# Slot lists of a GNN kernel: the prefix sum folds its columns twice, GpSimd subtracts the pairs of keys and clears two buffers

## The reference

```python
edge_index = jnp.stack([src, dst])
x = _layernorm(x + _L0_gnn_ref(x, edge_index, edge_weight, ...))        # GCN
x = _layernorm(x + _L1_gnn_ref(x, edge_index, edge_type_8, ...))        # gated, 2 rounds, 8 edge types, GRU
x = _layernorm(x + _L2_gnn_ref(x, edge_index, ...))                     # attention, 8 heads
x = _layernorm(x + _L3_gnn_ref(x, edge_index, edge_attr_64, ...))       # message MLP, mean over a node's edges
```

## Time and profile before

| | us |
|---|---|
| median of 3 runs | 11,153.66 |
| the profiled execution | 11,158.11 |
| its span | 11,156.3 |
| VectorE busy | 5,403.2 (48% of the span) |
| PE busy | 6,170.2 (55%) |
| ScalarE busy | 1,478.6 (13%) |
| GpSimd busy | 4,854.9 (44%) |

### The profile page before, as it was taken

How to read it: one execution, slowest core, us unless ns; L and a number is a source line. 1 busy time by engine, 2 the same in 40 slices (tenths; PEclk the granted TensorE clock), 3 DMA queues, 4 the chain that set the end, 5 groups by cost and what they waited for, 6 DMA issues and landing times. The chain is left out here.

```text
span 11156.3 us, 168161 instructions
## 1 busy us (share of the span) xinstructions
PE 6170.2 (55%) x61543; PEld 5314.1 (48%) x61544; DVE 5403.2 (48%) x7212; ACT 1478.6 (13%) x4112; POOL 4854.9 (44%) x5699
## 2 busy tenths in 40 slices
PE   4666659995433333343333333576899625554554
PEld 3333339994233233333333333575899624444444
DVE  7888878884311111121222222798888643323333
ACT  3666640000100000000000000121000011101111
POOL 1111100001277777767777777001000027777775
PEclk7777779997666666666666666555999857777777
DMA  1000032222222222222222121564322112222222
GB/s 45 0 0 0 0 50 81 85 82 88 81 66 65 53 65 66 65 71 53 52 52 52 52 52 52 190 258 181 107 93 91 60 44 71 78 79 78 78 78 72
DMA packets 323557, 804.89 MB, mean 72 GB/s; under 512 B 157650, under 2 KB 196348, under 8 KB 303772
## 3 DMA queue, kind: packets, MB, share of 16 engines
q1 hardware_dynamic: 148380, 429.92, 11.5%
q0 software_dynamic: 153216, 312.49, 10.8%
q10 hardware_dynamic: 21888, 61.54, 1.4%
HBM read 721.60 MB, written 81.99 MB: 72 GB/s over the span
## 5 line engine op out<-in xcount | busy, mean ns | idle before, releaser
L973 POOL DMA_INDIRECT ggnn_edges_G<-trans_d,ggnn_edges_rid x3136 | 2983.3, 951 | 1318.0 <-issue 955.6
L1077 PE MATMUL ggnn_edges_PS<-ggnn_edges_OH,ggnn_edges_G 128*128 128x128 f32 x6272 | 1177.3, 373 | 2323.9 <-DMA ggnn_edges_G<-trans_d,ggnn_edges_rid 2213.7
L1077 PEld LDWEIGHTS ggnn_edges_PS<-ggnn_edges_OH,ggnn_edges_G 128*128 128x128 f32 x6272 | 1137.0, 284 | 2368.8 <-issue 2368.8
L973 POOL DMA_INDIRECT mpnn_edges_G<-msg_d,mpnn_edges_rid x1568 | 1500.6, 957 | 741.2 <-issue 474.1
L1042 DVE TENSOR_TENSOR acc<-acc,ggnn_edges_PS 128x128 f32 x224 | 64.7, 289 | 2518.1 <-PE ggnn_edges_PS L1077 2518.1
L618 ACT ACTIVATE prep_OJF<-prep_OJ,prep_fld 128x98 bf16<-128x98 bf16 x3136 | 849.0, 362 | 575.2 <-DVE prep_OJ L674 575.2
L1061 PE MATMUL mpnn_edges_PS<-wt_late,mpnn_edges_at 128*128 128x256 f32 x1568 | 545.0, 521 | 681.0 <-DVE mpnn_edges_G L1029 338.4
L1061 PEld LDWEIGHTS mpnn_edges_PS<-wt_late,mpnn_edges_at 128*128 128x128 f32 x1568 | 414.7, 272 | 792.5 <-DVE mpnn_edges_G L1029 359.0
L822 PE MATMUL prep_PS<-prep_OJF,prep_OHr 128*128 128x490 bf16 x1582 | 582.5, 550 | 225.7 <-DVE prep_OHr L701 225.7
L1029 DVE TENSOR_TENSOR mpnn_edges_G<-mpnn_edges_G,mpnn_edges_PS 128x1792 f32<-128x1792 f32 x112 | 226.3, 2021 | 878.4 <-DMA mpnn_edges_G<-msg_d,mpnn_edges_rid 696.1
L1007 DVE SCALAR_TENSOR_TENSOR ggnn_edges_OH<-dstI,ggnn_edges_itm,ggnn_edges_PS 128x896 f32<-128x896 f32 x448 | 491.6, 1144 | 230.4 <-issue 164.7
(11 more groups left out here) (449 smaller groups left out, 10511.7 us busy)
## 6 DMA issues: line engine op xcount, KB each, us to landing
ba_rows<-slot_d SPq DMA_DIRECT2D x50, 3136.0 KB, 11.3
HB<-slot_d SPq DMA_DIRECT2D x50, 1568.0 KB
heads_rows<-slot_d SPq DMA_DIRECT2D x50, 1568.0 KB
ggnn_edges_G<-trans_d,ggnn_edges_rid POOLq DMA_INDIRECT x3136, 2.5
mpnn_edges_at<-in_edge_attr SPq DMA_DIRECT2D x112, 448.0 KB, 4.1
trans_d<-gcn_edges_tb ACTq DMA_DIRECT2D x49, 512.0 KB, 2.6
trans_d<-ggnn_edges_tb ACTq DMA_DIRECT2D x49, 512.0 KB, 3.0
mpnn_edges_G<-msg_d,mpnn_edges_rid POOLq DMA_INDIRECT x1568, 2.5
```

The lines of the kernel that those rows point to most:

```text
L973: pool.indirect_dma_start(G[:, s, c, :], None, table, bass.IndirectOffsetOnAxis(ap=rid[:, s, c:c + 1].bitcast(U32), axis=0)).then_inc(gath ...
L1077: mm = pe.matmul(wp[s % 2], G[:, s, c, :], OH[:, s % 2, c, :], start=c == 0, stop=c == GC - 1)
```

## The change

- The `twin` comparison is split. GpSimd subtracts each pair of keys (14 x 14, f32 out of bf16), after VectorE has signalled `key2` through the new semaphore `keyed`; `key2` has two buffers for that. VectorE then does the comparison with zero and the mask in one instruction and the sum in another, in a new function `same_key`, called at the end of the item, behind `window_hot`. Both are `own.step`.
- The reduce over 98 columns is preceded by two additions in place, of columns 50 to 97 onto 0 to 47 and of 26 to 49 onto 0 to 23, both bf16; the reduce then reads 26 columns.
- GpSimd clears `OJF` and `X` at the start of the stage. ScalarE, PE and VectorE wait for `fields_blank`, VectorE for `recs_blank` as well.

```diff
--- before.py
+++ after.py
@@ -508,7 +508,7 @@
             wm = sb(ctx, "prep_wm", [P, 2, 4, GC], BF16)
             w2 = sb(ctx, "prep_w2", [P, 2, 3, GC, 2], BF16)
             fld = sb(ctx, "prep_fld", [P, 2, 2, GC])
-            key2 = sb(ctx, "prep_key2", [P, GC, 2], BF16)
+            key2 = sb(ctx, "prep_key2", [P, 2, GC, 2], BF16)
             win = sb(ctx, "prep_win", [P, GC], I32)
             twin = sb(ctx, "prep_twin", [P, GC, GC])
             lower = sb(ctx, "prep_lower", [P, GC, GC])
@@ -544,8 +544,11 @@
             product, done, chain, final, turned, dsq, rooted, tidy, hscaled, stored, listed, filled, copied, cleared, over_ready = sems(
                 "prep", "product done chain final turned dsq rooted tidy hscaled stored listed filled copied cleared over_ready")
             totalled, slots_out, begun, taken = sems("prep", "totalled slots_out begun taken")
-            KEY_STEPS, RANK_STEPS, ADD_STEPS = 5, 6, 2
-            STEPS = KEY_STEPS + RANK_STEPS + ADD_STEPS
+            fields_blank, recs_blank = sems("prep", "fields_blank recs_blank")
+            keyed, diffed = sems("prep", "keyed diffed")
+            KEY_STEPS, RANK_STEPS, ADD_STEPS = 2, 8, 2
+            SAME_STEPS = 2
+            STEPS = KEY_STEPS + RANK_STEPS + ADD_STEPS + SAME_STEPS
             with nc.Block() as block:
                 @block.sync
                 def _(sp):
@@ -575,6 +578,8 @@
 
                 @block.gpsimd
                 def _(pool):
+                    nc.gpsimd.memset(OJF[:], 0.0).then_inc(fields_blank, 1)
+                    nc.gpsimd.memset(X[:], 0.0).then_inc(recs_blank, 1)
                     pool.wait_ge(zeroed, 1)
                     n = pool.value_load(turns_to[0:1, NCH:NCH + 1], min_val=1, max_val=KCAP // SL)
                     with pool.Fori(0, n) as i:
@@ -601,11 +606,17 @@
                                                   over(FLD[:, ds(g, 1), 2:5, :].rearrange("p g f c -> p (g f c)"), 2))
                             nc.gpsimd.tensor_copy(wm[:, par, 0:3], fg[:, 2:5, :]).then_inc(posted, 1)
                             pool.wait_ge(posted, k + 1)
+                            pool.wait_ge(keyed, k + 1)
+                            passed(pool, tick)
+                            nc.gpsimd.tensor_tensor(out=twin[:], in0=over(key2[:, par, :, 0], GC), in1=rows(key2[:, par, :, 0], GC),
+                                                    op=ALU.subtract).then_inc(diffed, 1)
+                            pool.wait_ge(diffed, k + 1)
                             passed(pool, tick)
 
                 @block.scalar
                 def _(act):
                     act.wait_ge(zeroed, 1)
+                    act.wait_ge(fields_blank, 1)
                     n = act.value_load(turns_to[0:1, NCH:NCH + 1], min_val=1, max_val=KCAP // SL)
                     with act.Fori(0, n) as i:
                         for s in range(SL):
@@ -633,9 +644,7 @@
                     own = Chain(dve, begun)
                     own.step(V.memset(itm[:], 0))
                     own.step(V.memset(acc[0:4, :], 0.0))
-                    own.step(V.memset(X[:], 0.0))
                     own.step(V.memset(OJ[:], 0.0))
-                    own.step(V.memset(OJF[:], 0.0))
                     own.step(V.memset(cnt[:], 0.0))
                     own.step(V.memset(RK[:], 0.0))
                     own.step(V.memset(within[:], 0.0))
@@ -651,6 +660,8 @@
                     dve.sem_inc(wdone, 2)
                     dve.sem_inc(hotd, 2)
                     dve.sem_inc(place_free, 1)
+                    dve.wait_ge(fields_blank, 1)
+                    dve.wait_ge(recs_blank, 1)
 
                     def pairs(a2, n):
                         return a2.unsqueeze(2).to_broadcast([P, GC, n // 2, 2])
@@ -667,16 +678,13 @@
                         dve.wait_ge(posted, k + 1)
                         dve.wait_ge(hot_key, k + 2)
                         own.step(V.tensor_single_scalar(win[:], off[:, par], 7, op=ALU.arith_shift_right))
-                        own.step(V.scalar_tensor_tensor(out=key2[:], in0=over(win[:], 2), scalar=MISS, in1=over(kk[:, par], 2),
+                        own.step(V.scalar_tensor_tensor(out=key2[:, par], in0=over(win[:], 2), scalar=MISS, in1=over(kk[:, par], 2),
                                                         op0=ALU.mult, op1=ALU.add))
+                        dve.sem_inc(keyed, 1)
                         dve.wait_ge(scaled, k + 1)
                         dve.wait_ge(wdone, k + 1)
-                        V.tensor_tensor(out=halves(OJ[:, par]), in0=pairs(key2[:], BK), in1=same_rows(iob[:, 0:BK], BK),
+                        V.tensor_tensor(out=halves(OJ[:, par]), in0=pairs(key2[:, par], BK), in1=same_rows(iob[:, 0:BK], BK),
                                         op=ALU.is_equal).then_inc(hot_key, 1)
-                        own.step(V.tensor_tensor(out=twin[:], in0=over(key2[:, :, 0], GC), in1=rows(key2[:, :, 0], GC),
-                                                 op=ALU.is_equal))
-                        own.step(V.tensor_tensor(out=twin[:], in0=twin[:], in1=lower[:], op=ALU.mult))
-                        own.step(V.tensor_reduce(within[:, par], twin[:], AX, ALU.add))
                         assert own.n - n0 == KEY_STEPS
 
                     def places(s):
@@ -696,7 +704,9 @@
                         dve.wait_ge(hot_key, k + 3)
                         own.step(V.tensor_tensor(out=halves(prod[:]), in0=halves(OJ[:, par]), in1=same_rows(pfx[:], BK),
                                                  op=ALU.mult))
-                        own.step(V.tensor_reduce(rank[:], prod[:], AX, ALU.add))
+                        own.step(V.tensor_tensor(out=prod[:, :, 0:48], in0=prod[:, :, 0:48], in1=prod[:, :, 50:BK], op=ALU.add))
+                        own.step(V.tensor_tensor(out=prod[:, :, 0:24], in0=prod[:, :, 0:24], in1=prod[:, :, 26:50], op=ALU.add))
+                        own.step(V.tensor_reduce(rank[:], prod[:, :, 0:26], AX, ALU.add))
                         own.step(V.tensor_tensor(out=rank2[:], in0=over(rank[:], 2), in1=over(within[:, par], 2), op=ALU.add))
                         V.tensor_tensor(out=halves(OHr[:, par]), in0=pairs(rank2[:], P), in1=same_rows(iob[:], P),
                                         op=ALU.is_equal).then_inc(hot_rank, 1)
@@ -726,6 +736,12 @@
                             ins = V.tensor_tensor(out=halves(OJF[:, par, :, 2 + a, :]), in0=halves(OJ[:, par]),
                                                   in1=pairs(w2[:, par, a], BK), op=ALU.mult)
                         ins.then_inc(wdone, 1)
+
+                    def same_key(k, s, own):
+                        dve.wait_ge(diffed, k + 1)
+                        own.step(V.scalar_tensor_tensor(out=twin[:], in0=twin[:], scalar=0.0, in1=lower[:],
+                                                        op0=ALU.is_equal, op1=ALU.mult))
+                        own.step(V.tensor_reduce(within[:, s % 2], twin[:], AX, ALU.add))
 
                     def window_hot(k, s):
                         par = s % 2
@@ -747,6 +763,7 @@
                             last = now
                             weigh_keys(k, s)
                             window_hot(k, s)
+                            same_key(k, s, own)
                         assert own.n == SL * STEPS
                         passed(dve, tick)
                     own = Chain(dve, chain)
@@ -832,6 +849,7 @@
                         mm.then_inc(product, 1)
 
                     pe.wait_ge(zeroed, 1)
+                    pe.wait_ge(fields_blank, 1)
                     pe.matmul(prefix, zero[:], zero[:, 0:BK], start=True, stop=True)
                     pe.matmul(total, zero[:], zero[:, 0:BK], start=True, stop=True).then_inc(prefix_ready, 1)
                     pe.matmul(placed[0], zero[:], OJF[:, 0, 0].rearrange("p f b -> p (f b)"), start=True, stop=True
```

## The result

The changed kernel takes 11,365.22 us (median of 5 runs, 11,362.27 to 11,365.77), before it was 11,153.66. The ratio is 1.0189, 95% interval 1.0178 to 1.0200: 212 us slower. Forecast were 11,390 us and slower. The way and the place came out as worked out; the sum was 25 us too high (33 us on the profiled executions, +237 for +204), most of it in one term.

What follows compares the result with a forecast made beforehand. VectorE's instruction stream was taken to set the slot-list loop's pace. Items summed to +250 us, memsets -13, together +237 on the profiled 11,158.1; from the 11,153.7 median, forecast 11,390 us, range 11,335 to 11,460.

Steps and rivals of the forecast that it cites:

- (a): Behind line 674's one-hot on VectorE: the pair comparison's three instructions and gaps go, saving 1.29 us an item.
- (b): sem_inc(keyed) between key2 and line 674: one semaphore step and two waits cost +0.11 to +0.26 us an item, taken +0.20.
- (c): The two folds and shorter reduce behind line 697: 1.48 us against 1.62, saving 0.14 an item.
- The fast rate: Folds run at line 697's bf16 rate, 0.50 and 0.33 us; at line 678's slow rate a loss of 0.41.
- (d): same_key's two instructions at the item's end: 0.69 us from line 733's end to the reduce's end, GpSimd's difference long ready.
- (e): Register loads behind the new reduce lose their cover: line 669 +2.92 us later within a turn, +4.07 at its end.
- (f): GpSimd's subtraction beside VectorE's line 674: VectorE held 0 or 0.5 us depending on which starts first, taken 0.25 an item.
- (g): Two memsets at the stage's start moved from VectorE to GpSimd: gain between 14 and 4 us, taken 13.
- The rival that would have been faster: Queue before line 669: register loads stay hidden, -0.46 us an item, 11,090 us with the memsets; chance 0.09.
- The slower one: Small terms in the loop go against it, GpSimd first or folds slow: 11,418, 11,452 or, both, 11,480 us; chance 0.14.

## Why the prediction was right

By its own steps, an item within a turn unless said otherwise:

- (a) Line 701 starts 0.08 ahead of line 686's end: 1.29 us saved, as put.
- (b) The gap ahead of the one-hot is 0.23 for 0.04: +0.19, taken +0.20. The run with `keyed` behind the one-hot gives these 21 us back by its profile, 17 by its time.
- (c) Folds 0.51 and 0.34, reduce 0.53: from line 705's end to line 710's start 1.52 for 1.65. The fast rate held.
- (d) From line 749's end to the reduce's end 0.67, taken 0.69. GpSimd's difference was never late.
- (e) The large term. The hole is mostly 2.07 to 2.22 us, in the mean 2.12, taken 2.15, and 4.53 at a turn's end, taken 4.54; with (d) it is +2.87 and +4.04 for the forecast's +2.92 and +4.07, 5 us less in all. The prediction's range gave this term no bounds. The added wait alone makes +282 us and the moved call takes about 262 back, so cause and size are shown from both sides.
- (f) *This term failed in its size.* I put 0.25 us, 28 us in all, between all and nothing. VectorE's one-hot was first in all 112 items, by about 0.01 us, took its usual 873 to 875 ns, and the hold cost nothing there. Nothing in the rows told the order beforehand; that it fell to the cheap side is luck. In the other order, with GpSimd let go ahead, VectorE was held, by 0.19 us where I had worked out 0.5 as the bound. A hold that I had not seen is some 0.05 us on the addition of line 710 in 84 of its 113 times (242 ns for 186, 5 us in all), while GpSimd's lines 602 and 603 run, which the subtraction has pushed back to there.
- (g) 10.6 us, taken 13; the other 1.3 by which the first item is earlier lie ahead of the stage. I had GpSimd through by 119 to 125 and let nothing of VectorE's wait for it but the items. Its cast, 0.23 us, stood until the second memset ended at 122.7, which took back 3.3 of the 13.9 us that the two memsets and the gaps around them had cost.

Without (f) the forecast's sum is 11,153.7 + 222 - 13 = 11,362; measured are 11,365. That they lie this close is in part luck: on the profiled executions it is +209 for +204, and the small misses above partly cancel. The prediction also gives (b) a bound of 0.09 us to both sides, but its rows and its sum have 0.06 upward, and no row is named for the 17 us by which the range is widened downward. The result needs neither. The rival that would have been faster (loads that stay hidden) fell: no load starts ahead of the reduce's end. The slower one fell with (f)'s order and (c)'s rate. The work that the change took from VectorE was saved, 71 us of busy time, 63 of them in the loop, and it counted: an item within a turn is 1.29 + 0.13 us shorter by (a) and (c). But the hole that the new order opens costs twice that.

## What to carry to other kernels

Register loads and semaphore steps are free only as long as the queue runs ahead under instructions that nothing waits for; put those last, right ahead of the loads, and every waited-for instruction in front of them: here that one choice made 262 us. When an instruction is moved, ask not only what it costs there but what the queue was doing behind it. For two engines that hold each other, the order of their starts decides who pays: signal the other one behind the long instruction, not ahead of it, which here also hid the step (0.19 us an item).

## What was not expected of the hardware

- The order of two starts 0.006 to 0.013 us apart came out the same way in 112 of 112 items. Of a race on paper one can't take the mean of both cases.
- A GpSimd memset, which has no input, held a VectorE cast (3.57 us for 0.23), while VectorE's memsets ran beside it at their usual length (RK 1.36 us in both kernels).
- GpSimd clears 13,720 bf16 elements in 11.53 us and the same bytes as 6,860 f32 in 5.82: the time goes by elements, 0.84 to 0.85 us a thousand.
- A register load takes 0.30 us and has 0.19 us of register work behind it; from one load to the next it is 0.6 to 0.75 us (1005.4, 1006.1 and 1006.8 in the item shown). Here three in a row are bare within a turn, six at each turn's end.
